# Attention scores computed a second time with keys as rows, in place of transposed probabilities, in a decoder block on one core

## The reference

```python
x = x + attn(layernorm(x))          # x: (4, 512, 512), 16 heads of 32, causal, with q/k/v/o weights and biases
x = x + xattn(layernorm(x), ctx)    # queries: the normed x itself; keys and values: ctx; 16 heads, causal, no weights
x = x + ffn(layernorm(x))           # relu(x @ W_up.T) @ W_down.T + sum(softmax(top-2 gate logits)) * (x @ W_expert)
# both attentions, per head: softmax(q @ k.T / sqrt(32), causal) @ v
```

## Time and profile before

| what | value |
|---|---|
| time, median of 3 runs (lowest to highest) | 816.69 us (815.62 to 818.06) |
| the profiled execution's own time | 816.02 us |
| its span, first to last instruction | 814.1 us |
| mean granted TensorE clock | 0.952 |
| GpSimd, its busiest shape (scaling) | 132.4 us of 255.5 |

### The profile page before, as it was taken

The page is one execution under the profiler, slowest core; times in us unless marked ns, Lnnn a source line. Parts: engine busy times, 40 slices in busy tenths (PEclk is TensorE's granted clock), DMA queues, the critical chain, the costliest instruction groups (busy, mean ns, idle before and its releaser), DMA issues.

```text
span 814.1 us, 14482 instructions
## 1 busy us (share of the span) xinstructions
PE 718.2 (88%) x4480; PEld 538.7 (66%) x4480; DVE 505.9 (62%) x1726; ACT 517.2 (64%) x1450; POOL 255.5 (31%) x390
## 2 busy tenths in 40 slices
PE   4997998979989899897789776899987999899998
PEld 3765676757766677675557544677765777667776
DVE  5466557656566565756556667766778667664532
ACT  6567676657766577666756777677667776675020
POOL 3634343334444344534630573301021112000100
PEclk9998899999999999999779898799999999999999
DMA  9542433225433353225654676333435353420001
GB/s 320 121 130 54 115 79 79 60 67 159 115 69 79 91 167 93 65 67 143 197 140 96 190 200 156 73 91 91 127 88 144 85 132 76 120 51 1 18 35 52
DMA packets 45995, 86.16 MB, mean 106 GB/s; under 512 B 8416, under 2 KB 8416, under 8 KB 45920
## 3 DMA queue, kind: packets, MB, share of 16 engines
q1 hardware_dynamic: 45920, 85.25, 40.0%
HBM read 27.55 MB, written 7.34 MB: 43 GB/s over the span
## 4 chain that ended last, share of the span: by engine, by line
PE 66%; DVE 12%; issue 8%; ACT 8%; POOL 4%; DMA 1%; DVEq 0%; SPq 0%; POOLq 0%; ACTq 0%
PE t L382 14%; PE m L412 11%; PE m L413 11%; PE m L414 11%; PE pv L406 10%; PE s L370 6%; DVE probs L558 3%; ACT probs L770 3%; POOL probs L872 3%; ACT prob L779 2%; DVE stats L585 2%; DVE prob L568 1%; PE m L425 1%; POOL w_lo L912 1%; PE pv L513 1%
## 5 line engine op out<-in xcount | busy, mean ns | idle before, releaser
L770 ACT ACTIVATE probs<-probs,negmax 128x128 f32<-128x128 f32 (+3 forms) x512 | 286.1, 559 | 138.9 <-DVE negmax L558 132.7
L558 DVE CUSTOM_DVE_ANT_0 probs<-s,mask 128x128 f32<-128x128 f32 (+3 forms) x512 | 247.0, 486 | 170.5 <-PE s L370 168.1
L382 PE MATMUL t<-ident,probs 128*128 128x128 f32 x1280 | 240.3, 290 | 66.8 <-ACT prob L779 53.6
L382 PEld LDWEIGHTS t<-ident,probs 128*128 128x128 f32 x1280 | 162.7, 146 | 144.2 <-ACT prob L779 84.1
L370 PE MATMUL s<-stack 96*128 96x128 f32 (+3 forms) x512 | 207.4, 408 | 0.0
L872 POOL TENSOR_SCALAR probs<-probs,rsum 128x128 f32<-128x128 f32 (+3 forms) x256 | 132.4, 536 | 217.6 <-DVE rsum L572 212.0
L779 ACT ACTIVATE prob<-t 128x512 f32<-128x512 f32 (+1 forms) x256 | 135.6, 530 | 82.6 <-PE t L382 82.3
L568 DVE COPY prob<-t 128x256 f32<-128x256 f32 (+1 forms) x256 | 91.2, 356 | 28.6 <-PE t L382 27.7
L370 PEld LDWEIGHTS s<-stack 96*128 96x128 f32 x512 | 103.0, 201 | 7.5 <-issue 0.5
L770 ACT ACTIVATION_READ_ACCUMULATOR probs<-probs,negmax 128x1 f32 x512 | 96.3, 188 | 0.0
L406 PE MATMUL pv<-prob,V 128*32 128x512 f32 (+3 forms) x1024 | 83.4, 470 | 0.0
(11 more groups left out here) (126 smaller groups left out, 902.1 us busy)
## 6 DMA issues: line engine op xcount, KB each, us to landing
stack<-stage SPq DMA_DIRECT2D x384, 128.0 KB, 2.3
xt<-in_x SPq DMA_DIRECT2D x16, 256.0 KB, 4.5
xres<-in_x SPq DMA_DIRECT2D x4, 1024.0 KB, 5.9
kraw<-in_ctxT SPq DMA_DIRECT2D x16, 256.0 KB, 2.9
V<-in_ctx SPq DMA_DIRECT2D x4, 1024.0 KB, 6.2
x<-xres SPq DMA_DIRECT2D x3, 1024.0 KB, 4.6
res<-x SPq DMA_DIRECT2D x8, 256.0 KB, 5.4
out<-res SPq DMA_DIRECT2D x2, 1024.0 KB, 4.4
```

The costliest lines, as they stand in the source:

```text
L382: mm = nc.tensor.transpose(dst[:, chunk(qb - kb)], probs[:, (2 * P + h) % 3, OFF[qb] + PART * kb:OFF[qb] + PART * kb + PART], ident[:, :])
L558: nc.vector.tensor_tensor_reduce(probs[:, (2 * P + h) % 3, OFF[qb]:OFF[qb + 1]], score_tile(P, i), mask[:, T - N:T], -SCALE, BIG, ALU.add, ...
L770: nc.scalar.activation(tile, tile, ACT.Exp, bias=negmax[:, P % 2, h, qb:qb + 1], scale=-1.0, accum_out=total).then_inc(p_exp, 1)
```

## The change

Each score tile is computed twice. The first pass is as before and only serves the maximum: `top_of` writes the masked tile back to its PSUM bank, of which there are now two. The unscaled negated maxima of a head (128 queries x 4 blocks) are split into high and low halves (`split_max`, VectorE), transposed by PE (`turn_max`, into a bank `xb`), copied to SBUF (`max_out`, ScalarE) and laid by a DMA (`load_max`) into two further rows of `stack`, beside two rows of ones. The second pass (`scores_turned`) takes keys as the stationary side and queries as the moving one over 98 rows, so the maximum is subtracted in the matmul and the tile comes out with keys as rows. Its eight pieces of a pair are packed into five 512-wide tiles; ScalarE takes the exponential of each from PSUM to `PT` in SBUF (`exped`), GpSimd zeroes what lies above the diagonal (`cut`), and `values` reads `PT`. No transposes, copies of them, or scaled probabilities remain.

The sums of a row now come from PE: a matmul of ones against `PT` (`sums`), which gives the sum on all 32 partitions of a head. In the groups of `PLAIN` (16 to 21) all of `PT` streams; in the others GpSimd first adds the key blocks (`add_up`) and 512 columns stream. Self-attention: VectorE takes the reciprocal of 128x512 in four pieces (`recip`), GpSimd multiplies (`scaled`), ScalarE adds the value bias and rounds (`context`), GpSimd makes the low half (`context_lo`). Cross-attention transposes the sums back beside the values.

Scores are issued in step P (before: P - 1), the second pass in steps P + 1 and P + 2, values in step 2G + 4, sums three slots later. The norms move from VectorE to ScalarE; the feed-forward weights' high halves from GpSimd to ScalarE. The gate's matmuls and transposes use 8 rows in place of 128. `FIRST` is -2 (before: -4), `FEED` starts at steps 45, 53, 61 and 69, and `plan` gets new slots.

```diff
-FIRST = -4
+FIRST = -2
-NS, NTB = 3, 2
-FEED = (PAIRS * 42 + 4, PAIRS * 51 + 4, PAIRS * 60, PAIRS * 67 + 4)
+NS, NST = 2, 2
+RP = 3
+TILES = 5
+TILE_SLOT = ((1, 3), (1, 5), (1, 7), (2, 1), (2, 2))
+MAX_SLOT = ((0, 5), (1, 1))
+PLAIN = range(NGS, NGS + 6)
+FEED = tuple(PAIRS * (NPS + 13 + PAIRS * f) for f in range(B))
...
+            def load_max(P, h):
+                sp.wait_ge(mx_out, 2 * P + h + 1)
+                need(sp, st_mm, TILES * (P - RP + 1))
+                sp.dma_start(f32(stack[RS:XS, P % RP, h, 0, :]), f32(mxT[0:2 * NT, h, :])).then_inc(mx_in[P % RP][h], 16)
...
+                if 0 <= s - 1 < NP:
+                    load_max(s - 1, 1)
+                if 0 <= s + 1 < NP:
+                    load_stack(s + 1)
+                if 0 <= s < NP:
+                    load_max(s, 0)
...
-            def turn(P, i):
+            def scores_turned(P, j):
+                if j in (0, 2):
+                    pe.wait_ge(mx_in[P % RP][j // 2], 16 * (P // RP + 1))
+                need(pe, p_exp, TILES * P + j - NST + 1)
+                for h, kb in parts(j):
+                    at = place(h, kb)[1]
+                    mm = nc.tensor.matmul(turned_bank(P, j)[:, at:at + T - PART * kb], stack[0:XS, P % RP, h, 1, chunk(kb)],
+                                          stack[0:XS, P % RP, h, 0, PART * kb:T], start=True, stop=True)
+                mm.then_inc(st_mm, 1)
...
+            def sums(G):
+                pe.wait_ge(cn_done, G + 1)
+                if G in PLAIN:
+                    for kb in range(NT):
+                        for j in range(4):
+                            mm = nc.tensor.matmul(pv_bank[HD * j:HD * j + HD, PART * kb:T], ones[:, :],
+                                                  prob_of(2 * G + j // 2, j % 2, kb), start=(kb == 0), stop=(kb == NT - 1))
+                else:
+                    for j in range(4):
+                        nc.tensor.matmul(pv_bank[HD * j:HD * j + HD, 0:PART], ones[:, :],
+                                         prob_of(2 * G + j // 2, j % 2, 0)[:, 0:PART], start=True, stop=True)
+                    pe.wait_ge(acc_done, added_up(2 * G + 1))
+                    for j in range(4):
+                        mm = nc.tensor.matmul(pv_bank[HD * j:HD * j + HD, PART:T], ones[:, :],
+                                              acc[:, j // 2, j % 2, :], start=True, stop=True)
+                mm.then_inc(sum_mm, 1)
...
+                nc.vector.tensor_tensor_reduce(score_tile(P, i), score_tile(P, i), mask[:, T - N:T],
+                                               -1.0, BIG, ALU.add, ALU.min, negmax[:, P % 2, h, qb:qb + 1]).then_inc(s_max, 1)
+            def split_max(P, h):
+                dve.wait_ge(s_max, PAIRS * P + NT * (h + 1))
+                need(dve, mt_mm, 2 * (P - 1) + h + 1)
+                nc.vector.tensor_copy(mx[:, h, 0, :], negmax[:, P % 2, h, :]).then_inc(mx_hi, 1)
+                dve.wait_ge(mx_hi, 2 * P + h + 1)
+                nc.vector.tensor_tensor(mx[:, h, 1, :], negmax[:, P % 2, h, :], f32(mx[:, h, 0, :]), ALU.subtract)\
+                    .then_inc(mx_lo, 1)
+            def recip(G, q):
+                if q == 0:
+                    dve.wait_ge(sum_mm, G + 1)
+                    need(dve, cn_scaled, G)
+                nc.vector.reciprocal(rs[:, chunk(q)], pv_bank[:, chunk(q)]).then_inc(r_done, 1)
...
+            def exped(P, j):
+                act.wait_ge(st_mm, TILES * P + j + 1)
+                if j == 0 and P >= RP:
+                    act.wait_ge(sum_mm, (P - RP) // 2 + 1)
+                nc.scalar.activation(PT[:, P % RP, j, :], turned_bank(P, j)[:, :], ACT.Exp, scale=SCALE).then_inc(p_exp, 1)
...
+            for r in range(RP):
+                for h in range(2):
+                    nc.scalar.activation(stack[RS:XS, r, h, 1, :], ones[RS:XS, 0:1].broadcast_to([XS - RS, T]), ACT.Copy)\
+                        .then_inc(ones_row, 1)
...
+            def add_up(P):
+                nc.gpsimd.tensor_tensor(total, ring[:, 0:3:2, PART:T], ring[:, 1:4:2, 0:T - PART], ALU.add).then_inc(acc_done, 1)
+                pool.wait_ge(acc_done, done + 1)
+                nc.gpsimd.tensor_tensor(total[:, :, PART:], total[:, :, PART:],
+                                        ring[:, 4, :].rearrange("p (h n) -> p h n", h=2), ALU.add).then_inc(acc_done, 1)
+                pool.wait_ge(acc_done, done + 2)
+                nc.gpsimd.tensor_tensor(total[:, :, 2 * PART:], total[:, :, 2 * PART:], ring[:, 1:4:2, T - PART:T],
+                                        ALU.add).then_inc(acc_done, 1)
```

More of the change, by code:

```diff
@@ L125, in plan @@
         n = free.index(min(free))
-        assert free[n] <= z
+        assert free[n] <= z, (z // 8, z % 8, key, free, last)
         bank_of[key], before[key] = n, last[n]
@@ L514, in back @@
                 mm.then_inc(c_mm, 1)
+                pe.wait_ge(mx_out, min(2 * (2 * G + 4) + 1, 2 * NP))
+                for t in range(NT):
+                    mm = nc.tensor.transpose(x_bank[:, chunk(t)], rs[:, chunk(t)], ident[:, :])
+                mm.then_inc(ct_mm, 1)
             def turn_gate(f):
@@ L519, in turn_gate @@
                 for t in range(NT):
-                    mm = nc.tensor.transpose(dst[:, chunk(t)], lg[:, chunk(t)], ident[:, :])
+                    mm = nc.tensor.transpose(dst[:, NE * t:NE * t + NE], lg[0:NE, chunk(t)], ident[0:NE, 0:NE])
                 mm.then_inc(gate_t, 1)
-            pe.wait_ge(made, 5)
+            pe.wait_ge(made, 6)
             for t in range(NT):
@@ new lines, in _ @@
+                    if s % 2 == 0 and 0 <= s // 2 - 2 < NG and i == 2:
+                        raw_values(s // 2 - 2)
+                    for j, (later, slot) in enumerate(TILE_SLOT):
+                        if i == slot and 0 <= s - later < NP:
+                            exped(s - later, j)
+                    if s % 2 == 0 and NGS <= s // 2 - 2 < NG and i == 4:
+                        raw_sums(s // 2 - 2)
+                    if s % 2 == 1 and 0 <= (s - 5) // 2 < NGS and i == 2:
+                        context((s - 5) // 2)
@@ L858, in _ @@
+                    if s % 2 == 1 and NGS <= (s + 3) // 2 < NG and i == 4:
                         query_hi((s + 3) // 2)
+                    for j in range(1, 2 * B):
+                        if z in norm_slots(j):
+                            norm(j, norm_slots(j).index(z))
                     for f in range(B):
-                        if z == feed_start(f) + TURN_AT + 3:
+                        if 0 <= z - f_norm_slot(f) < NT:
+                            f_norm(f, z - f_norm_slot(f))
+                        if z == FEED[f] + TURN_AT + 3:
@@ L944, in _ @@
                 b, p = divmod(s, PAIRS)
-                if 0 <= s < NPS:
-                    for qb in range(NT):
-                        scaled(s, 1, qb)
-                if s % 2 == 1 and NGS <= (s - 3) // 2 < NG:
-                    added((s - 3) // 2)
-                if s % 2 == 0 and NGS <= s // 2 + 2 < NG:
-                    keys(s // 2 + 2)
+                if 0 <= s - 2 < NP:
+                    cut(s - 2, 2)
+                for f in range(B):
+                    if s == FEED[f] // PAIRS - 1:
+                        f_scale(f)
@@ new lines, in _ @@
+                if s % 2 == 1 and 0 <= (s - 5) // 2 < NGS:
+                    scaled((s - 5) // 2)
+                if s % 2 == 1 and NGS <= (s - 5) // 2 < NG:
+                    added((s - 5) // 2)
+                if 0 <= s - 2 < NP:
+                    cut(s - 2, 3)
+                    cut(s - 2, 4)
+                if 0 <= s - 1 < NP:
+                    cut(s - 1, 0)
+                if 0 <= s - 2 < NP and (s - 2) // 2 not in PLAIN:
+                    add_up(s - 2)
+                if s % 2 == 1 and 0 <= (s - 5) // 2 < NGS:
+                    context_lo((s - 5) // 2)
@@ L976, in _ @@
-                if 0 <= s + 1 < NPS:
-                    for qb in range(NT):
-                        scaled(s + 1, 0, qb)
+                    if 0 <= s - SPLIT_AT[n] < KC:
+                        f_split_lo(n, slot, s - SPLIT_AT[n])
 def kernel(**inputs):
```

582 lines of the change are left out of this document (305 added, 277 removed).

## The result

The changed kernel takes 882.5 us (median of 4 runs, 879.2 to 883.5), the one before 816.7 (815.6 to 818.1) beside it: a ratio of 1.080, 95% interval 1.077 to 1.083. The forecast was 785, the range ended at 828. The profiled execution has a span of 881.8 us and a mean clock of 0.925 (before 0.952).

What follows compares the result with a forecast made beforehand. PE, busy 88%, was taken as the bound, with stalls the part that could fall. Start 30.4 + self-attention 349 + bare steps 116 + feed-forward 225 + tail 63 = 783.4, + 1.9 outside = 785.3; forecast 785 us, range 738 to 828.

Steps and rivals of the forecast that it cites:

- I take 1.4 of stall: Self-attention steps: PE stalls 1.4 us beside 9.5 of work, so 10.9 a step, 349 over 32 steps.
- The reciprocals: Self-attention on VectorE: 128x512 in four pieces, 3.2 us a group, 1.6 a step; bounds 0.69 and 3.2 a group.
- The lock: VectorE's small split passes held by GpSimd's two-input operations through the shared SBUF port: 1.2 us a step, bounds 0 and 4.
- VectorE is then held 9.6 of each self-attention step: VectorE's 8.4 us of work and waits with 1.2 of port holds, in the queue of the maxima that free score banks.
- The round through ScalarE and GpSimd leaves the path: Self-attention: this round no longer delays PE, VectorE's bursts with two banks come in; stall taken as 1.4, now 1.65.
- Together 7.1 of an 11 us step. It fits: GpSimd's cuts 1.9, additions 3.9 and 512-wide operations 1.3 us a step were said to fit in the step.
- Bare steps 8.1 each: Cross-attention steps 32 to 44: 13 steps of 8.1 us (ring and VectorE, against 5.7 of PE work).
- the clock rival: Bare steps: half of steps 29 to 44 run at 1.2 GHz, costing 20 us more, total 805; chance 0.12.
- Feed-forward steps 10.7: Steps 45 to 65: PE work 9.8 in place of 9.9, stall as now, 10.7 x 21 = 225 us.
- VectorE behind a locked port: PE waits on maxima behind VectorE: self-attention steps 12.2, feed-forward 11.3, total 847; slower once self-attention passes 11.7; chance 0.20.
- Stalls nearly gone: Splits fall between GpSimd's additions, second-pass banks give slack: self-attention and feed-forward steps 10.2, total 739; chance 0.23.
- if the splits are mostly locked: Sign of being wrong: VectorE's 128x4 copies and differences, 0.09 to 0.17 us unlocked, mostly locked at up to 2.

Runs made afterwards that it cites:

- x2: The changed kernel with a plain copy in place of each self-attention reciprocal; 850.0 us.
- x5: The changed kernel with the maximum split after its transpose, low half read from PSUM, two small DMAs a head in place of one; 854.8 us.
- x18: The changed kernel with only GpSimd's queue reordered: context's low half ahead of the additions, layer-norm's four small operations at the head of their step; 863.2 us.
- x1: The changed kernel without GpSimd's three additions a step, PE reading a buffer of ones in their place; 846.6 us.
- x3: The changed kernel with both GpSimd's additions left out and a copy in place of each reciprocal; 801.8 us.
- x10: x5 with a copy in place of each reciprocal, additions kept; 833.9 us.
- x11: The changed kernel without first score pass and maximum (743.5 us), with a minimum with 1.0 in place of each reciprocal; 744.8 us.
- x6: The changed kernel with both score passes and all maxima, but maxima unused: no split, transposes, copies or DMAs, second pass over 96 rows; 833.8 us.
- x8: x5 with the self-attention reciprocal moved to ScalarE as exp(-ln); 868.1 us.

## Why the prediction was wrong

**The step that failed** is the stall of a self-attention step, "I take 1.4 of stall". PE's own work came out as forecast: the start-to-start times at the full clock are 0.233 us for a 512-wide matmul of the second pass and 0.24 and 0.76 a group for the sums, and with every pair of neighbouring matmuls at its own fast distance (the 15th to 25th percentile of its kind in this stage) a step is 9.2 to 9.4 us, forecast 9.5. Against 13.16 that leaves 3.7 or more of stall. The 24 steps between G=2 and 14 are 54 us over the forecast; to G=2 (115.4 against 30.4 + 8 x 10.9 = 117.6) nothing is. Three things are in it, which the prediction had priced and then let lie beside other work (the first two) or had put at nothing (the third). Between G=2 and 14 x2 took 21.2 us, x5 14.8 and x18 17.3, together 53.3 of the 54; no run has all three at once, and x1 to x3 show that such parts need not add up exactly.

- **The reciprocals**, forecast 0.88 a piece and 3.2 us a group, measured 0.949 a piece with the next instruction starting 0.87 after, 3.5 a group. The size was nearly right (the 5.8 ns an element of the earlier trace rows carried to 128). Copies in their place take 43 us of VectorE's work; that is worth 32.5 us of time in the change (x2), 21 beside x5 (x10) and, without maxima, nothing (x11). The Trainium skill's repeat count of 8 ("VectorE: DVE Perf Modes", First, the fixed hardware budget) gave an estimate of 4.3 a group; the trace has 3.5.
- **The lock**, forecast 1.2 a self-attention step, measured 25.4/24 = 1.1 there and 52/64 = 0.8 over all steps. Again the VectorE time was no underestimate; x5, which takes it away, is 27.7 us faster, net of the two waits that it adds. Additions account for 28 of the 52 us, and the context multiplication for much of the rest in self-attention. The mistake was to read "VectorE is then held 9.6 of each self-attention step" against 10.9 as room. It was busy only 209.88/24 = 8.7, and PE waited 79 us of the kernel for its maxima and splits: with two banks each score matmul needs the maximum of the tile two before it, and a burst in front of one can be a stall whatever the step's total.
- **GpSimd's order**, forecast as nothing: "The round through ScalarE and GpSimd leaves the path". Its longest wait left PE's list, but GpSimd's part came back at the end of a batch, where layer-norm's scalars and the context's low half stand behind the additions; 19 us (x18). "Together 7.1 of an 11 us step. It fits" was right (178.36/24 = 7.4) and no argument: what counts is what stands behind a 3.9 us block, and that was not looked up.

**The other terms.** Bare steps 8.1 each: 129 us between G=14 and 20 and 0.80 of the clock. With 11 for the output projection the forecast for these 12 steps was 108, so 21 us are over it. PE stands idle there for 25.3 us, 2.1 a step, which is no more than the forecast's 8.1 - 5.7. With each pair of neighbouring matmuls at its fast distance (the 15th percentile in the whole kernel) PE's work is 66.7 us, 5.6 a step, as forecast. The other 37 us are matmuls further apart than that, at a mean clock of 0.80: with levels of 2.4 and 1.2 GHz, two fifths of the stretch were at the lower one. So the clock rival, which priced 20 us here, fits this term, though no run changes the clock alone. Eight late reciprocals are in front of maxima there (x2 took 2.5), and x6 took 6.4. Feed-forward steps 10.7: 11.6, 20 us over 22 steps. The term took "stall as now" and had no lock in it, which is 0.6 of the 0.9 (x5); 0.3 are left over the forecast. Tail 63: 66.2. Start 30.4: the first scores are at 31.4. After G=2 every stage came out longer than forecast, so no two errors of the sum cancel.

**The rivals.** "VectorE behind a locked port" (847, chance 0.20) was the case that came, by the trigger it named (a self-attention step over 11.7), 35 us too low. Without GpSimd's order it is 863 (x18); of the 16 us that remain, 10 are in bare steps and 10 in feed-forward steps, 3 in the tail, and the part up to G=14 is 7 below that rival's own sum. "Stalls nearly gone" and the forecast both took ScalarE's relief as PE's; ScalarE did fall to 41%, and PE's waits for its copies did go. Of the signs listed, that of being wrong ("if the splits are mostly locked") does not hold by count: the median cast takes 0.17 us, and 16 of 128 take over 1.2. The few long ones make most of the 52 us. By the prediction's own list the chance of faster is 0.45 + 0.23 + 0.9 x 0.12 = 0.79, where it wrote 0.77.

## What to carry to other kernels

When work moves to an engine that has room, list what stands behind each new block in that engine's queue and when it is due; 19 us went on one 1.3 us operation of the context and four small ones of layer-norm, which could simply be issued first. What an addition to an in-order engine costs depends on what stands behind it: the same reciprocals cost 32 us where the bounding engine waits for what follows them, and nothing where it does not. Keep small SBUF passes of VectorE off the critical ring when GpSimd is given long two-input operations, or read an operand from PSUM. And when a leave-out run gives the time that its theory had, look whether it also removed what the theory named: x1 removed about half of it.

## Not expected of the hardware

- A 4-element cast on VectorE took 1.76 us beside a 1.82 us addition on GpSimd, against 0.16 alone; a subtraction of 4x128 with one operand in PSUM took 275 ns on average and 0.28 us at most beside the same additions.
- Ln and Exp in turns on ScalarE brought a table load of 1283 ns before each, two a group. The Trainium skill ("ScalarE: Activation LUTs", Table sets: the hidden batching unit) counts one load for a logarithm and an exponential behind it, as one set holds both; the trace of x8 doesn't agree.
- Reading the accumulated maximum takes 140 ns in the changed kernel and 83 in the one before. The changed one's maximum pass writes to PSUM and its mask is bf16; no run tells which of the two it is. The instruction behind starts no later for it: 0.34 us after the start of a 256-wide pass in both.
- Two score banks in place of three made the kernel before 0.6% faster, which no run explains.
